# Moving half of an output product out of a two-bank accumulator rotation and into an otherwise idle bank, in four pieces

## The reference, cut to what matters

```python
def _L0_xattn_ref(x, context, Wq, Wk, Wv, Wo, bo):       # x (16, 256, 256), context (16, 77, 192)
    ...                                                  # 16 heads of 64, Wq (256, 1024), Wo (1024, 256)
    sim = jnp.einsum('bhid,bhjd->bhij', q, k) * SCALE
    attn = jax.nn.softmax(sim, axis=-1)
    out = jnp.einsum('bhij,bhjd->bhid', attn, v)
    out = out.transpose(0, 2, 1, 3).reshape(B, Nq, INNER_DIM)
    return out @ Wo + bo
...
x = x + _L0_attn_ref(_layernorm(x, axis=-1), ...)        # windows of 8 tokens
x = x + _L0_xattn_ref(_layernorm(x, axis=-1), ctx_768, ...)
x = x + _L0_ffn_ref(_layernorm(x, axis=-1), ...)         # router, argmax, eight gated experts
```

## Time and profile before

| | |
|---|---|
| median of three runs (lowest to highest) | 1324.24 us (1318.14 to 1330.51) |
| the profiled execution | 1317.3 us |
| its span, first to last instruction | 1315.2 us |
| mean granted TensorE clock | 0.97 |
| busy: TensorE, its weight loads, VectorE, ScalarE, GpSimd | 91%, 75%, 65%, 45%, 50% |

### The profile page before, as it was taken

The page is one execution under the profiler, slowest core; times in us unless marked ns, Lnnn a source line. Parts: engine busy times, 40 slices in busy tenths (PEclk is TensorE's granted clock), DMA queues, the critical chain, the costliest instruction groups (busy, mean ns, idle before and its releaser), DMA issues. The chain is left out here.

```text
span 1315.2 us, 22142 instructions
## 1 busy us (share of the span) xinstructions
PE 1196.4 (91%) x8032; PEld 985.0 (75%) x8032; DVE 854.6 (65%) x1501; ACT 596.8 (45%) x987; POOL 652.0 (50%) x541
## 2 busy tenths in 40 slices
PE   5999798999898999999999999935999999999996
PEld 2656466776676777677767777735999999999996
DVE  3688346767556776557774334326788888888883
ACT  1243422544414445313544443414566666666662
POOL 6357217466547374475583222224355555555552
PEclk9999898999998999989999999967999999999998
DMA  8433301111120101201114211005676666666650
GB/s 179 125 116 116 94 15 42 44 28 44 33 61 8 44 20 44 51 11 28 34 35 132 44 45 36 17 17 178 216 247 235 226 213 215 216 215 236 219 176 3
DMA packets 95382, 133.46 MB, mean 101 GB/s; under 512 B 42394, under 2 KB 76908, under 8 KB 89411
## 3 DMA queue, kind: packets, MB, share of 16 engines
q1 hardware_dynamic: 79299, 111.30, 27.2%
q0 software_dynamic: 16000, 21.07, 5.9%
HBM read 113.04 MB, written 24.73 MB: 105 GB/s over the span
## 5 line engine op out<-in xcount | busy, mean ns | idle before, releaser
L1750 PE MATMUL psH<-xhigh,whigh 128*128 128x256 f32 x736 | 209.7, 285 | 8.1 <-DVE wlow L1598 6.7
L1750 PE MATMUL psH<-xlow,whigh 128*128 128x256 f32 x736 | 207.4, 282 | 0.0
L1750 PE MATMUL psH<-xhigh,wlow 128*128 128x256 f32 x736 | 207.4, 282 | 0.0
L1598 DVE TENSOR_TENSOR wlow<-staged,whigh 128x2048 fp32r<-128x2048 f32 x69 | 157.9, 2290 | 0.0
L1750 PEld LDWEIGHTS psH<-xhigh,whigh 128*128 128x128 f32 x736 | 141.6, 192 | 8.7 <-issue 6.9
L1667 ACT ACTIVATE whigh<-staged 128x2048 fp32r<-128x2048 f32 x69 | 132.3, 1919 | 25.7 <-PEq L137 15.9
L1136 PE MATMUL psA<-xT,wq 128*128 128x256 f32 x512 | 130.1, 405 | 11.9 <-ACT xT L625 11.9
L1750 PEld LDWEIGHTS psH<-xlow,whigh 128*128 128x128 f32 x736 | 140.7, 191 | 0.0
L1750 PEld LDWEIGHTS psH<-xhigh,wlow 128*128 128x128 f32 x736 | 140.5, 191 | 0.0
L1492 POOL TENSOR_TENSOR idle<-e_less 128x1 f32<-128x1 f32 x42 | 49.7, 1182 | 169.9 <-DVE ys L1625 90.6
L1269 PE MATMUL psD<-vo,pT 128*128 128x128 f32 x1024 | 131.6, 276 | 0.3
(11 more groups left out here) (214 smaller groups left out, 2629.2 us busy)
## 6 DMA issues: line engine op xcount, KB each, us to landing
staged<-in_L_ffn_w SPq DMA_DIRECT2D x69, 1024.0 KB, 5.0
tokens<-out_rows POOLq DMA_DIRECT2D x32, 256.0 KB, 7.2
kT<-k_cols SPq DMA_DIRECT2D x16, 308.0 KB, 2.9
vo<-v_rows SPq DMA_DIRECT2D x16, 308.0 KB
xb<-in_x SPq DMA_DIRECT2D x32, 128.0 KB
b2s<-in_L_ffn_b SPq DMA_DIRECT2D x23, 128.0 KB, 2.6
k_cols<-qT SPq DMA_DIRECT2D x4, 616.0 KB
v_rows<-pT SPq DMA_DIRECT2D x4, 616.0 KB
```

The costliest lines, as they stand in the source:

```text
L1598: tt(wlow[par][:, i, :], staged[:, i, :], whigh[par][:, i, :].bitcast(F32), ALU.subtract)\
L1750: ins = mm(psH[:, q % 2 * PAIR + c, part, :], lhs, rhs, start=i == 0, stop=i == len(passes) - 1)
```

## The change

X2b no longer has a place in `D_ORDER`: psD's rotation is 20 uses per sequence instead of 21. It accumulates in bank 0 of psW instead, with two semaphores of its own (`x2_full` from TensorE, `x2_done` from VectorE), and its eight matmuls are issued in four pieces: 0 and 1 between XN2' and Q0', 2 before the last pair of rough scores, 3 to 5 before NM', 6 and 7 before RANK. Around the pieces there are new waits: for the read of the last X2b before bank 0 is written again, at b = 0 and b = 3 for the window attention's last use of bank 0, and before the window attention's own first use for `x2_done`. VectorE's order is the same; `residual2(1)` reads psW and signals `x2_done`.

```diff
 D_ORDER = ([f"PV{v}" for v in range(8)] + ["PROJ'", "X2a", "LOG"] + [f"MAX{m}'" for m in range(8)]
-           + ["X2b", "RANK"])
+           + ["RANK"])
...
             def residual2(half, g, j, b, last):
 
-                ps, value = full("X2a" if half == 0 else "X2b", j, b, last)
+                if half == 0:
+                    ps, value = full("X2a", j, b, last)
+                    done = d_done
+                else:
+                    dve.wait_ge(x2_full, j + 1)
+                    ps, value, done = psW[:, 0, :], j + 1, x2_done
...
+            def output_second(us, j):
+
+                for u in us:
+                    ins = mm(psW[:, 0, 0:C], o2T[:, u, P:2 * P], wo[:, u, :], start=u == 0, stop=u == CH - 1)
+                if us[-1] == CH - 1:
+                    ins.then_inc(x2_full, 1)
...
                         if more and b == 0 and v == 0:
+                            if j > 0:
+                                pe.wait_ge(x2_done, j)
                             window_turn(n, 0)
                             window_turn(n, 1)
...
                             if more and b == 3:
+                                pe.wait_ge(x2_done, j)
                                 output_turn(n, v // 2 - 1)
...
                     if not last:
                         turn_normed(xn, "XN2'", j, b, normed2, j + 2)
+                    if j > 0:
+                        pe.wait_ge(x2_done, j)
+                    if more and b == 0:
+                        pe.wait_ge(wd_done, n * WD_ITEMS + 12)
+                    if more and b == 3:
+                        pe.wait_ge(wa_done, n * WA_ITEMS + 9)
+                    output_second([0, 1], j)
+                    if not last:
                         queries(0, j, b)
                         for q in range(1, 4):
                             queries(q, j, b)
                             scores_for_max(q - 1, j, b)
+                    output_second([2], j)
+                    if not last:
                         scores_for_max(3, j, b)
-                    output_product(1, j, b, last, lambda: None if last else turn_maxima(j, b))
+                    output_second([3, 4, 5], j)
+                    if not last:
+                        turn_maxima(j, b)
+                    output_second([6, 7], j)
```

More of the change, by code:

```diff
@@ L252, in trunk @@
         k_in, v_in = sem("k_in"), sem("v_in")
+        x2_full, x2_done = sem("x2_full"), sem("x2_done")
         ids_cleared, id_ready = sem("ids_cleared"), sem("id_ready")
@@ L908, in residual2 @@
                 mine = out_rows[:, b % 2, half, C:2 * C]
-                then(dve, tt(mine, ps[:, 0:C], x1[:, b % 2, half], ALU.add), d_done, value)
+                then(dve, tt(mine, ps[:, 0:C], x1[:, b % 2, half], ALU.add), done, value)
                 carry_waits()
@@ L1199, in _, with output_first @@
             turn_maxima(-1, -1)
-            def output_product(half, j, b, last, between):
-                ps = freeD("X2a" if half == 0 else "X2b", j, b, last)
+            def output_first(j, b, last):
+                ps = freeD("X2a", j, b, last)
                 for u in range(CH):
-                    if half == 0 and u % 2 == 0:
+                    if u % 2 == 0:
                         take_a(f"O{u // 2}", j, b, last)
-                    if u == CH // 2:
-                        between()
-                    ins = mm(ps[:, 0:C], o2T[:, u, half * P:(half + 1) * P], wo[:, u, :], start=u == 0, stop=u == CH - 1)
+                    ins = mm(ps[:, 0:C], o2T[:, u, 0:P], wo[:, u, :], start=u == 0, stop=u == CH - 1)
                 ins.then_inc(d_full, 1)
+            def output_second(us, j):
[3 more added lines that the diff above has]
+                    ins.then_inc(x2_full, 1)
             def logits(name, j, b, last):
@@ L1319, in turn @@
                         turn_output2(3)
-                    output_product(0, j, b, last, lambda: None)
+                    output_first(j, b, last)
                     if first:
```

## The result

| | before | changed |
|---|---|---|
| median (lowest to highest) | 1328.21 us (1318.14 to 1332.36), 6 runs | 1290.07 us (1289.34 to 1294.82), 6 runs |
| profiled execution, its span | 1317.3, 1315.2 | 1294.82, 1292.7 |
| mean granted clock in it | 0.970 | 0.974 |

The ratio is 0.9743, 95% interval 0.9706 to 0.9779. On another chip later, with both kernels side by side, it was 1293.28 against 1323.73, ratio 0.9770 (0.9747 to 0.9793).

A forecast was written before the change was run, and what follows sets the result against it. TensorE, busy 91% of the span, was taken as the bound, with only its stalls to win. Nine ends at 1.5, three at 0.9 and three at 0.35 gave 17.2 us, so 1307 us from 1324.24; range 1297 to 1317.

The forecast's parts named there:

- An ordinary end: Nine sequence ends (b = 1 and b = 3 of the first three groups, three in the last group): 1.5 us saved each.
- The late start of Q0': At an ordinary end, the queries start up to 0.1 us later because matmuls 0 and 1 precede them.
- pieces 3 to 5: X2b matmuls before NM', no longer waiting for a psD bank, start at about 449.1 instead of 449.40: 0.3 us saved.
- b = 2: Three ends where `choose` is slow beside GpSimd's product: RANK gains 0.2, VectorE 0.5; 0.35 us taken for each.
- the new wait of RANK for `onehotb`: At b = 2 RANK's place comes before `onehotb` is ready, so it waits about 1.3 us.
- b = 0: Three ends at the half clock: 1.56 less 0.5 for late queries and 0.15, leaving 0.9 us saved each.
- piece 2: One X2b matmul before the last rough scores; at b = 0 it pushes them by 0.1 to 0.2 us.
- my second rival: Filling the hole at b = 0 brings the full clock back sooner: gain 23 us, 1301 us; chance 0.16.
- it lies 6.9 under the median of the runs: The profiled execution, 1317.3 us, against the median 1324.24; the 17.2 us saving was taken off that median.
- The borders rival: Each piece pays up to 0.10 us at each of five borders, 15 ends: gain 9.7, 1314.5 us; chance 0.17.
- The drain: Leaving psW and returning drains TensorE's array at five borders, 15 ends, costing 27 us: 1334 us; chance 0.05.
- `choose` delaying RANK elsewhere than at b = 2: Sign of being wrong: waits for `onehotb` outside b = 2; an ordinary end was expected clear by 0.4 us.

The follow-up runs named there:

- the leave-one-out kernels: Two variants of the changed kernel: no X2b matmul before the last rough scores, 1296.58 us; no X2b matmuls before the queries, 1308.32 us.
- bank_only: Changed kernel with X2b in the old order, four matmuls before the turned maxima and four behind, only the psD bank wait gone: 1312.60 us, ratio 0.9925.
- rank_later: Changed kernel with RANK of b = 2 moved behind the first four score rows of the next sequence: 1291.48 us, ratio 0.9763 to the kernel before.
- sums_first: Changed kernel with VectorE's order at b = 2 changed: a value sum and the residual before `choose`, RANK later: 1311.21 us, ratio 0.9900.
- before_dummy: Kernel before plus two thrown-away fp32 matmuls per end, between the turned rows and the first queries: 1315.84 us, ratio 0.9931.
- after_dummy_b0: Changed kernel plus four thrown-away fp32 matmuls before the turned rows at b = 0 of the first three groups: 1291.78 us, ratio 0.9760 to the kernel before.
- before_again: Kernel before, unchanged, run again with another execution profiled: 1321.40 us, ratio 1.0001.
- before_dummy_tail: Kernel before plus two thrown-away fp32 matmuls per end, between X2b and RANK where TensorE has no hole: 1330.25 us, ratio 1.0047.

## Why the prediction was wrong, step by step

**Direction and mechanism** were right: each piece went into a hole, the waits for the bank are gone, no engine became late but VectorE at b = 2, where I had expected it, and nothing went slower.

**An ordinary end: 1.72 instead of 1.5 us.** The terms were 0.86 - 0.1, 0.43 and 0.3; the leave-one-out kernels and bank_only measure 0.88, 0.43 and 0.41. The late start of Q0' that I took off does not exist (1.40 us behind the transposes in both kernels), and pieces 3 to 5 start sooner than my 0.3 allowed. Nine ends: 15.5 instead of 13.5.

**b = 2: 0.46 instead of 0.35**, with the new wait of RANK for `onehotb` (1.35 us, forecast about 1.3). rank_later adds what I had only touched: even without that wait VectorE holds b = 3 back. The Trainium skill's rule ("SBUF — State Buffer", section "Who interferes with whom") fits what sums_first shows: the blocking follows the GpSimd product, not the line. One of the instructions it caught there is a cast with one input; the rule names casts too, in a two-port mode.

**b = 0: the step that failed.** I let the clock return at the same moment as before, took off 0.5 us for a late Q0' and 0.15 for piece 2, and kept 0.9 us an end. Measured 4.32, 3.05 and 3.07. Q0' was 0.08 us later, not 0.5 to 0.9. At the end of j = 4, where the clock stayed up in before_dummy and in after_dummy_b0, the period is 38.81 in the one and 37.10 in the other: the order saves 1.71 here as well. The rest of each saving, 1.3 to 2.6, is the clock. This was my second rival, given 0.16: the queries took 4.72 instead of 6.15 us, and at j = 0 the clock did not fall in that execution.

**The step that was missing.** I put the saving of one profiled execution on the median of all, "it lies 6.9 under the median of the runs", and did not ask why it lies there. It was before with the fewest low stretches. In other executions the clock also falls at b = 2 and b = 3, behind stops that the change fills or shortens (before_again). The median therefore held a second cost, put at nothing in my sum, that the trace of before did not show (34.1 us of low time in before_again against its 20.5), and that the change removes as well.

The account on one chip, for 1323.73 - 1293.28 = 30.5 us: order 12 x 1.72 + 3 x 0.46 = 22.0; clock, from 0.967 to 0.972 on average, 16 us less at half clock at 0.50 to 0.56 each, 8 to 9. Together 30 to 31. On the first chip the gap of the medians was 38 us; how much of it was clock there isn't known, since the clock of its six timed executions of before was not recorded. An estimate: executions of before that took 1328 to 1330 us on the other chips had a clock of 0.964 or 0.965. With 0.964 against the 0.974 of the changed kernel it is 28 us less at half clock, 14 to 16 us, and with the order 36 to 38.

**The borders rival** (1314.5) is out: leaving out the piece of one matmul costs 0.43 and leaving out that of two 0.88, their own lengths, with nothing left for borders. **The drain** (1334) is out the same way: the open group in psW costs nothing that these periods show while other banks are written in between. `choose` delaying RANK elsewhere than at b = 2 did not happen, though only 0.27 us were left at j = 5.

Open: what exactly tips the clock. The experiments show that filling one hole raises its mean over the executions (before_dummy, after_dummy_b0) and that the same work elsewhere helps less (before_dummy_tail), not which stop at b = 2 or b = 3 is the one.

## What to carry to other kernels

Where TensorE is the bound, price a hole twice: the time it stands, and what the half clock costs behind it in the executions where it falls. Matmuls thrown away in a hole are a quick test of the second part. One profiled execution shows one draw of the clock: before putting its saving on a median, compare its granted clock with that of the other runs. And a small VectorE instruction that sits beside long GpSimd ones is not moved safely by its data dependencies alone: look at what GpSimd runs at the new place.

## What the runs showed of the hardware that I had not expected

- A kernel with 30 more fp32 matmuls, all thrown away, was 0.7% faster (0.9906 to 0.9956), its granted clock 0.973 instead of 0.967.
- The 29 executions of one kernel on one core lie between 1317.6 and 1329.1 us, and go with the mean granted clock: 1319.3 us on average at 0.970, 1327.5 at 0.964.
- VectorE instructions of 0.17 us took 2.17, 2.44 and 3.63 us beside a GpSimd product of 3.9 us with two SBUF inputs, and ended within 0.1 us of it.
- An accumulation group of eight fp32 matmuls left open in one bank through three other streams in other banks cost no measurable time (the pieces saved 0.43 and 0.88 us, the length of one and of two matmuls).
